# Edge counts by (source block, target) keys in a two-layer graph kernel: pairs of 32-target windows in place of single 64-target windows

## The chip, the cores and the metric

The kernel runs on one core of one Trainium2 chip. The metric is the device time of one execution in microseconds (us). Differences of about 0.2% are what a measurement of this kernel can tell from no change.

## The reference, cut to what matters

There are 1024 nodes with 512 features and 16384 edges `src -> dst`, sorted by `dst`. The targets are drawn as 1024·u², so low numbers of `dst` are the crowded ones; `src` is uniform.

```python
h = relu(layernorm(x))
adj = zeros((N, N)).at[src, dst].set(1)
a = (h @ Wq + bq) @ (h @ Wk + bk).T / sqrt(512)
x = x + softmax(a * adj + (1 - adj) * -1e6) @ (h @ Wv + bv)

h = relu(layernorm(x)) @ W1 + b1
deg = 1 + number of edges per dst;  dinv = deg ** -0.5      # loops included
agg(h)[s] = sum over edges and loops s -> d of dinv[s] * dinv[d] * h[d]
h = relu(batchnorm(agg(h), over nodes)) @ W2 + b2
x = x + agg(h)
```

Both layers need the N x N matrix of edge counts: the first as a mask with sources as rows, the second as the matrix of the aggregations, with targets on the contraction side.

## The kernel before, in words

**Counting.** The edges lie as 128 chunks of 128. The targets are cut into NW = 16 windows of WIN = 64, taken in `ORDER` (14, 15, 0, 1, ... 13). Since edges are sorted, a window needs a run of chunks, whose bounds the program computes into the table `lohi` and reads into a register (`value_load`, L660 on VectorE and L1010 on TensorE). For each chunk VectorE makes two one-hot tiles: `src_oh` (128 edges x 512 columns, L668; a source of 512 and over is told apart by its other tile) and `dst_oh` (L670, three chunks in one instruction: 2 x 64 columns, by half of the sources and target in the window). TensorE multiplies them and adds in PSUM (L1018). A **round** is three chunks (UNROLL) and fills one of 4 ring slots; a window is one lead round of two chunks and then a loop (`Fori`) of rounds whose number is known only from the register. `dst_oh` is compared against `drel`, one table for each window, which GpSimd makes (L355). ScalarE moves a finished window from PSUM to `cnt16` (targets as partitions) in two instructions, which sum the degrees as they go.

With these edges there are 149 chunk visits in 55 rounds: 16 lead rounds and 39 loop rounds. Window i = 2 (targets 0 to 63, "the big window" below) has the lead round and 11 loop rounds; windows i = 3 to 15 have 13 lead and 26 loop rounds.

**Items.** While counting goes on, TensorE also makes "items": h transposed, v, q, and others. The table `ahead` says which items stand before which window. An item is made in a PSUM bank by TensorE, its high part is copied by ScalarE, and VectorE writes the low part (`lo_of`, L651, L647). Matrix products are done as three passes (L948, L949, L950) of high and low parts.

**Attention and W1.** For 8 tiles of 128 sources: scores on TensorE, mask by `copy_predicated` (L768) over `adj`, a DMA transpose of `cnt16` through two rotating buffers, softmax, p split in two halves and transposed by DMA, p times v (`weighted_v`), second layer norm, times W1 (`times_w1`). `dinv` is computed by GpSimd (L314) right after counting.

**Aggregation and W2.** The counts are copied to f32 tiles `cnt` and multiplied with h in agg1 (L1119); batch statistics (L914 to L918), ReLU and the low part of z (L885); z times W2; agg2 (L1196). W2 has a tile of its own, `w2`, loaded by SP (L252) at the beginning of attention and split by ScalarE (L414) and VectorE (L636) near its end.

Each engine's instructions stand in a written order, with semaphores between engines; nothing is reordered by a scheduler.

## Time and profile before

| | before |
|---|---|
| median of 3 runs (lowest, highest) | 311.49 us (311.35, 312.01) |
| profiled execution | 311.82 us |
| its span | 309.8 us |
| mean granted TensorE clock | 0.999 |
| TensorE matmuls busy | 295.1 us (95%) |
| VectorE busy | 210.2 us (68%) |
| ScalarE busy | 143.6 us (46%) |
| GpSimd busy | 55.4 us (18%) |

The profiled execution's time is 2.0 us above its span: what lies before the first and after the last recorded instruction. Times below are us from the start of the span, and a "q" behind an engine's name (DVEq) is its sequencer: it runs the register, branch and table-reading instructions and hands the others on. Such instructions don't count as busy. DVE is VectorE, PE TensorE, ACT ScalarE, POOL GpSimd, SP the engine that issues most DMAs.

### The profile page before, as it was taken

To read this page: it belongs to the slowest core of one execution; us is meant where nothing else is said; L and a number is where in the kernel's file an instruction comes from. 1 tells how busy PE (TensorE), PEld (TensorE's weight loads), DVE (VectorE), ACT (ScalarE), POOL (GpSimd) and SP (SyncE) were. 2 spreads that over 40 slices of the span, in tenths; PEclk is the share of its full clock that TensorE was granted. 3 is DMA by queue.
4 is the path that set the end of the run, shared out by engine and by line. 5 is a ranking of instruction groups with operands and counts; after the bars stand their busy time and mean duration, and the time that the engine had idled before them with its cause. 6 is when DMAs were issued, how large, how long until landed. Compare 5 with 4: busy or idle time off the path is not lost.

```text
span 309.8 us, 4740 instructions
## 1 busy us (share of the span) xinstructions
PE 295.1 (95%) x1319; PEld 227.4 (73%) x1319; DVE 210.2 (68%) x470; ACT 143.6 (46%) x245; POOL 55.4 (18%) x96
## 2 busy tenths in 40 slices
PE   2999969899999999999999999999999999999995
PEld 2977436565666688888888888888788888888884
DVE  3787999999997747667647575757444288376311
ACT  1799944443445626635465445437632035233000
POOL 5234280000000170032121212203010043100000
PEclk9999999999999999999999999999999999999999
DMA  7707040000420127832834636133203000000221
GB/s 268 291 3 204 1 135 0 3 0 0 150 57 3 33 36 107 200 85 53 136 69 102 135 46 124 36 68 59 44 0 70 1 0 2 0 0 2 101 103 68
DMA packets 42310, 21.65 MB, mean 70 GB/s; under 512 B 35760, under 2 KB 36016, under 8 KB 42288
## 3 DMA queue, kind: packets, MB, share of 16 engines
q1 hardware_dynamic: 41744, 20.33, 26.9%
q10 hardware_dynamic: 544, 1.05, 0.9%
q8 instruction: 11, 0.18, 0.2%
q14 instruction: 11, 0.09, 0.1%
HBM read 10.88 MB, written 2.10 MB: 42 GB/s over the span
## 4 chain that ended last, share of the span: by engine, by line
PE 79%; DVE 10%; issue 4%; DVEq 4%; DMA 1%; ACT 1%; SPq 0%; ACTq 0%
PE ps L948 18%; PE ps L950 18%; PE ps L949 18%; PE ps L1196 9%; PE ps L1119 8%; PE ps L1018 5%; DVE src_oh L668 4%; PE ps L986 2%; DVEq L668 2%; DVE dst_oh L670 2%; DMA edge_i<-src_in 1%; DVE hT L651 1%; DVEq L670 1%; DVEq L660 0%; DVEq L674 0%
## 5 line engine op out<-in xcount | busy, mean ns | idle before, releaser
L668 DVE TENSOR_SCALAR src_oh<-iota,ecol 128x512 f16 x149 | 44.2, 346 | 4.0 <-issue 2.9
L1018 PE MATMUL ps<-src_oh,dst_oh 128*128 x149 | 37.9, 382 | 5.4 <-DVE dst_oh L670 4.6
L1018 PEld LDWEIGHTS ps<-src_oh,dst_oh 128*128 x149 | 14.4, 103 | 25.6 <-issue 16.7
L1119 PE MATMUL ps<-cnt,qh 128*128 128x512 f32 x128 | 30.1, 391 | 0.3 <-ACT cnt L541 0.3
L1196 PE MATMUL ps<-qh,cnt 128*128 128x512 f32 x128 | 29.3, 390 | 0.0
L443 ACT ACTIVATE cnt<-ps 64x512 int16<-64x512 f32 x32 | 18.9, 592 | 20.7 <-PE ps L1032 20.3
L1119 PEld LDWEIGHTS ps<-cnt,qh 128*128 128x128 f32 x128 | 23.9, 188 | 5.6 <-DVE qh L827 0.7
L1196 PEld LDWEIGHTS ps<-qh,cnt 128*128 128x128 f32 x128 | 23.9, 188 | 5.2 <-DVE vb L929 0.3
L950 PE MATMUL ps<-v,pT 128*128 128x512 f32 x64 | 25.0, 390 | 0.0
L948 PE MATMUL ps<-v,pT 128*128 128x512 f32 x64 | 24.9, 390 | 0.0
L949 PE MATMUL ps<-v,pT 128*128 128x512 f32 x64 | 24.9, 390 | 0.0
L948 PE MATMUL ps<-hT,qh 128*128 128x512 f32 x64 | 24.9, 389 | 0.0
L949 PE MATMUL ps<-hT,qh 128*128 128x512 f32 x64 | 24.9, 389 | 0.0
L950 PE MATMUL ps<-hT,qh 128*128 128x512 f32 x64 | 24.9, 389 | 0.0
L382 POOL TENSOR_SCALAR lnb<-bnag 128x1 f32<-128x1 f32 x8 | 8.2, 1028 | 82.2 <-DVE bnag L801 82.2
L941 DVE SCALAR_TENSOR_TENSOR xt<-ps,dinv,x 128x512 f32<-128x512 f32 x8 | 5.7, 747 | 17.1 <-PE ps L1196 17.1
L790 DVE TENSOR_SCALAR pT<-p16T 128x1024 fp32r<-128x1024 f16 x8 | 5.5, 693 | 15.9 <-DMA p16T<-p 15.8
L768 DVE COPY_PREDICATED T<-adj,ps 128x1024 f32<-128x1024 int16 x8 | 10.6, 1322 | 7.8 <-PE ps L950 7.8
L525 ACT ACTIVATE hnT<-h16T 128x512 fp32r<-128x512 f16 x8 | 5.1, 632 | 23.2 <-DMA h16T<-h 23.2
L497 ACT ACTIVATE T<-T,smx 128x1024 f32<-128x1024 f32 x8 | 9.2, 1150 | 13.1 <-DVE smx L773 13.1
L466 ACT ACTIVATE T<-zerob,fill 128x1024 f32<-128x1024 bf16 x8 | 9.1, 1147 | 11.9 <-DVE p L780 11.9
L670 DVE TENSOR_TENSOR dst_oh<-iota_w,drel_first 128x384 f16 (+1 forms) x35 | 14.4, 411 | 0.0
(176 smaller groups left out, 658.8 us busy)
## 6 DMA issues: line engine op xcount, KB each, us to landing
xt<-x_in SPq DMA_DIRECT2D x16, 256.0 KB, 3.3
out<-xt SPq DMA_DIRECT2D x8, 256.0 KB, 2.1
qk_raw<-L_gnn_Wk_in ACTq DMA_DIRECT2D x2, 512.0 KB, 4.9
qk_raw<-L_gnn_Wq_in SPq DMA_DIRECT2D x2, 512.0 KB, 6.7
wB_raw<-L_gnn_Wv_in SPq DMA_DIRECT2D x2, 512.0 KB, 8.9
wB_raw<-L_gnn_W_in SPq DMA_DIRECT2D x2, 512.0 KB, 4.3
w_raw<-L_gnn_W_in SPq DMA_DIRECT2D x2, 512.0 KB, 4.8
bias_row<-L_gnn_b_in SPq DMA_DIRECT2D x2, 256.0 KB, 3.7
```

Of the source, the lines that this page charges most:

```text
L443: act.activation(cnt16[rows, a * KC:(a + 1) * KC, w // 2, :], ps[a * WIN:(a + 1) * WIN, i % 2, :].rearrange("p (s n) -> p s n", n=P), ACT. ...
L466: act.activation(T[:, t % 2, :], zerob[:, 0:1].to_broadcast([P, N]), ACT.Identity, bias=fill[:, t:t + 1]).then_inc(S["mask_set"], 1)
L497: act.activation(T[:, t % 2, :], T[:, t % 2, :], ACT.Exp, bias=smx[:, 1, t:t + 1], scale=SCALE, accum_out=smx[:, 2, t:t + 1]).then_inc(S[" ...
L668: dve.tensor_scalar(src_oh[:, bass.ds(slot, 1), j, :].rearrange("p a n -> p (a n)"), iota[:, :], ecol[:, bass.ds(c + j, 1)], None, ALU.is_ ...
L670: dve.tensor_tensor(dst_oh[:, bass.ds(slot, 1), :, 0:count].rearrange("p a n u -> p (a n) u"), iota_w[:, :, 0:count], drel(i)[:, bass.ds(c ...
L768: dve.copy_predicated(T[:, t % 2, :], adj[:, t % ADJ, :], ps[:, 2 * (t % 2):2 * (t % 2) + 2, :].rearrange("p a n -> p (a n)")).then_inc(S[ ...
L948: pe.matmul(out_, stat(1), mov(0), start=first, stop=False)
L949: pe.matmul(out_, stat(0), mov(1), start=False, stop=False)
L950: return pe.matmul(out_, stat(0), mov(0), start=False, stop=last)
L1018: m = pe.matmul(ps[:, i % 2, :], dst_oh[:, bass.ds(slot, 1), :, j].rearrange("p a n -> p (a n)"), src_oh[:, bass.ds(slot, 1), j, :].rearra ...
L1119: m = pe.matmul(bank(g), qh[:, d, a, c * P:(c + 1) * P], cnt[:, d, n * HALF:(n + 1) * HALF], start=(d == 0 and a == 1), stop=last)
L1196: m = pe.matmul(bank(t), cnt[:, d, t * P:(t + 1) * P], qh[:, d, a, :], start=(d == 0 and a == 1), stop=last)
```

## The change

Windows become 32 targets wide, two of them form a pair, and a pair takes the place of a window (NW = 16 pairs, in the same order). The moving tile of a chunk is now `key_oh`, 128 x 256: key = (block of 128 sources) x 32 + target in the window, made with a subtraction and a comparison in one instruction. The stationary tile is `src_oh`, the source's place in its block, 128 columns for each of three chunks. There is no lead round, and no table `drel`; each of a pair's two windows has a loop of its own and bounds of its own. Each pair is moved by one ScalarE instruction of 128 x 512 into `cntT`, with sources as partitions, and the mask reads that directly. For the aggregations eight DMA transposes turn `cntT` into `cntD`. Degrees are summed by eight ScalarE instructions over `cntD` in tiles 1 and 2, and `deg`, the added loops and the flag follow on VectorE in tiles 3 to 5; `dinv` comes on GpSimd ahead of the third `ln2_coef`. W2 shares `wB` with Wv and W1, so it is loaded only when the last product with W1 is done, and is split behind that. The ring has 8 slots.

With the same edges there are now 183 chunk visits in 61 rounds, all of three chunks in loops: 4 in pairs i = 0 and 1, 12 in pair i = 2, and 45 in pairs i = 3 to 15.

```diff
-WIN = 64
-NW = N // WIN
-LEAD = 2
+WIN = 32
+NWIN = N // WIN
+PAIR = 2
+NW = NWIN // PAIR
+BLK = 8
+KEYS = BLK * WIN
 UNROLL = 3
 PAD = 4
-ROUNDS = NW * (2 + NCH // UNROLL)
-RING = 4
+ROUNDS = NWIN * (2 + NCH // UNROLL)
+RING = 8
...
+             [("q", 0, 1)], [("q", 0, 2), ("w", 0, 0)], [("q", 0, 3)], [], []]
...
-                sp.wait_ge(S["c16"], 2 * NW)
-            if t >= ADJ:
-                sp.wait_ge(S["masked"], t - ADJ + 1)
-            sp.dma_start_transpose(adj[:, t % ADJ, :].rearrange("p (b n) -> p b n", b=NT),
-                                   cnt16[:, t, :, :].rearrange("p b n -> p (b n)")).then_inc(
-                S[f"adj_in{t % ADJ}"], 16)
+                sp.wait_ge(S["c16"], NW)
+                sp.wait_ge(S["fill_ready"], 1)
+            sp.dma_start_transpose(cntD[:, :, t, :], cntT[:, t, :]).then_inc(S["turned"], 16)
...
+            if t == 0:
+                for u in range(KC, NT):
+                    turn_counts(u)
...
-            if t == 0:
-                load_w(2)
...
+        sp.wait_ge(S["w1_ps"], NT)
+        load_w(2)
...
+            if t == 2:
+                pool.wait_ge(S["deg_ready"], 1)
+                pw(dinv[:, :], deg[:, :], NT).then_inc(S["dinv_ready"], 1)
...
-            w = ORDER[i]
-            rows = slice(w % 2 * WIN, (w % 2 + 1) * WIN)
+            targets = slice(PAIR * WIN * ORDER[i], PAIR * WIN * (ORDER[i] + 1))
             act.wait_ge(S["c_done"], i + 1)
-            for a in range(2):
-                act.activation(cnt16[rows, a * KC:(a + 1) * KC, w // 2, :],
-                               ps[a * WIN:(a + 1) * WIN, i % 2, :].rearrange("p (s n) -> p s n", n=P), ACT.Copy,
-                               accum_out=degp[rows, a, w // 2:w // 2 + 1]).then_inc(S["c16"], 1)
+            act.activation(cntT[:, :, targets].rearrange("p b (w t) -> p w b t", w=PAIR),
+                           ps[:, i % 2, :].rearrange("p (w b t) -> p w b t", w=PAIR, b=BLK), ACT.Copy).then_inc(S["c16"], 1)
...
+        def degrees(blocks):
+            act.wait_ge(S["turned"], 16 * NT)
+            for b in blocks:
+                act.activation(cntD[:, b, :, :], cntD[:, b, :, :], ACT.Copy,
+                               accum_out=degp[:, b:b + 1]).then_inc(S["deg_sums"], 1)
...
+                degrees(range(KC))
...
+                degrees(range(KC, NT))
...
+        split_w(2)
...
+        step(dve.tensor_scalar(dst_low[:, :], edge_i[:, 0, :], WIN - 1, None, ALU.bitwise_and))
+        step(dve.scalar_tensor_tensor(out=steps[:, 0, :], in0=dst_low[:, :], scalar=1.0 / BLK - 1.0, in1=edge_i[:, 0, :],
+                                      op0=ALU.mult, op1=ALU.add))
...
+        step(dve.tensor_scalar(src_low[:, :], edge_i[:, 1, :], P - 1, None, ALU.bitwise_and))
+        step(dve.scalar_tensor_tensor(out=steps[:, 1, :], in0=src_low[:, :], scalar=-1.0, in1=edge_i[:, 1, :],
+                                      op0=ALU.mult, op1=ALU.add))
+        dve.scalar_tensor_tensor(out=edge_f[:, 0, :], in0=steps[:, 1, :], scalar=float(WIN) / (P * BLK), in1=steps[:, 0, :],
+                                 op0=ALU.mult, op1=ALU.add)
+        dve.tensor_copy(edge_f[:, 1, :], src_low[:, :]).then_inc(S["edge_f_ready"], 1)
...
         def bounds_of(i):
-            return dve.value_load(lohi[0:1, ORDER[i]:ORDER[i] + 1], min_val=256, max_val=257 * NCH)
...
+            return [dve.value_load(lohi[0:1, win:win + 1], min_val=256, max_val=257 * NCH)
+                    for win in (PAIR * ORDER[i], PAIR * ORDER[i] + 1)]
         def onehots(i, bounds):
...
+            for a in range(PAIR):
+                win = PAIR * ORDER[i] + a
+                with dve.Fori(bounds[a] & (NCH - 1), bounds[a] >> 8, UNROLL) as c:
+                    k = dve.snap(made, min_val=0, max_val=ROUNDS)
+                    slot = k & (RING - 1)
+                    dve.wait_ge(S["onehots_used"], k + 1)
+                    for j in range(UNROLL):
+                        dve.tensor_scalar(key_oh[:, bass.ds(slot, 1), j, :].rearrange("p a n -> p (a n)"), iota[:, :],
+                                          kcol[:, bass.ds(c + j, 1)], -float(KEYS * win), ALU.subtract, ALU.is_equal)
+                    dve.tensor_tensor(src_oh[:, bass.ds(slot, 1), :, :].rearrange("p a n u -> p (a n) u"), iota_s[:, :, :],
+                                      scol[:, bass.ds(c, UNROLL)].rearrange("p (o u) -> p o u", o=1).to_broadcast(
+                                          [P, P, UNROLL]), ALU.is_equal).then_inc(S["onehots"], 1)
+                    dve.reg_add(made, made, 1)
...
+        def degrees():
+            dve.wait_ge(S["deg_sums"], NT)
+            dve.tensor_scalar(deg[:, :], degp[:, :], 1.0, None, ALU.add).then_inc(S["deg_ready"], 1)
+            dve.wait_ge(S["deg_ready"], 1)
+            dve.tensor_reduce(degm[:, 0:1], deg[:, :], AX.X, ALU.max).then_inc(S["degm_ready"], 1)
...
-            dve.copy_predicated(T[:, t % 2, :], adj[:, t % ADJ, :],
+            dve.copy_predicated(T[:, t % 2, :], cntT[:, t, :],
...
+            if i == 3:
+                degrees()
+            if i == 4:
+                for b in range(NT):
+                    add_loops(b)
+            if i == 5:
+                large_flag()
...
+            if i == 3:
+                act.wait_ge(S["dinv_ready"], 1)
...
+        split_w(2, 0)
+        split_w(2, 1)
...
-            return pe.value_load(lohi[0:1, ORDER[i]:ORDER[i] + 1], min_val=256, max_val=257 * NCH)
...
+            return [pe.value_load(lohi[0:1, win:win + 1], min_val=256, max_val=257 * NCH)
+                    for win in (PAIR * ORDER[i], PAIR * ORDER[i] + 1)]
         def counts(i, bounds):
             if i >= 2:
-                pe.wait_ge(S["c16"], 2 * (i - 1))
...
+                pe.wait_ge(S["c16"], i - 1)
+            pe.matmul(ps[:, i % 2, 0:32], zerob[:, :], zerob[:, 0:32], start=True, stop=False, skip_group_check=True)
+            for a in range(PAIR):
+                with pe.Fori(bounds[a] & (NCH - 1), bounds[a] >> 8, UNROLL):
+                    k = pe.snap(used, min_val=0, max_val=ROUNDS)
+                    slot = k & (RING - 1)
+                    pe.wait_ge(S["onehots"], k + 1)
+                    for j in range(UNROLL):
+                        m = pe.matmul(ps[:, i % 2, a * KEYS:(a + 1) * KEYS],
+                                      src_oh[:, bass.ds(slot, 1), :, j].rearrange("p a n -> p (a n)"),
+                                      key_oh[:, bass.ds(slot, 1), j, :].rearrange("p a n -> p (a n)"), start=False,
+                                      stop=False, skip_group_check=True)
+                    m.then_inc(S["onehots_used"], 1)
+                    pe.reg_add(used, used, 1)
```

On VectorE, at the head of the first window (before) or pair (after); `lohi` is the table of bounds, ISA and REGISTER_ALU are register instructions, the tiles are the one-hot tiles above. Before:

```order
L660 TENSOR_LOAD lohi
L660 ISA x2
L664 ISA [waits drel_ready]
L668 REGISTER_ALU [waits onehots_used]
L668 ISA
L668 REGISTER_ALU
L668 ISA
L668 TENSOR_SCALAR src_oh<-iota,ecol 128x512
```

After:

```order
L651 TENSOR_LOAD lohi
L651 ISA x2
L651 TENSOR_LOAD lohi
L651 ISA x2
L658 REGISTER_ALU
L658 UNCONDITIONAL_BRANCH
L658 ISA
L663 REGISTER_ALU [waits onehots_used]
L663 ISA
L663 TENSOR_SCALAR key_oh<-iota,kcol 128x256
```

Bounds are read twice in place of once, the wait for `drel` is gone, and the one-hot tiles begin inside a loop. On VectorE, the body of such a loop, one round. Before:

```order
L668 REGISTER_ALU [waits onehots_used]
L668 ISA
L668 TENSOR_SCALAR src_oh<-iota,ecol 128x512
L668 ISA
L668 TENSOR_SCALAR src_oh<-iota,ecol 128x512
L668 ISA
L668 TENSOR_SCALAR src_oh<-iota,ecol 128x512
L670 ISA
L670 TENSOR_TENSOR dst_oh<-iota_w,drel_first 128x384
L674 ISA
L681 COMPARE_AND_BRANCH
```

After:

```order
L663 REGISTER_ALU [waits onehots_used]
L663 ISA
L663 TENSOR_SCALAR key_oh<-iota,kcol 128x256
L663 ISA
L663 TENSOR_SCALAR key_oh<-iota,kcol 128x256
L663 ISA
L663 TENSOR_SCALAR key_oh<-iota,kcol 128x256
L665 ISA
L665 TENSOR_TENSOR src_oh<-iota_s,scol 128x384
L668 ISA
L658 COMPARE_AND_BRANCH
```

The instructions are the same in number and kind, with half the columns in three of them. On VectorE, between the last product with W1 and the first aggregation result (`w` is `w2`, `vb` and `qh` are the parts of h that agg1 reads, `flag` tells of large counts). Before:

```order
L808 TENSOR_SCALAR hnT<-h16T 128x512 [waits w1_ps,h16_lo_in]
L636 TENSOR_TENSOR w<-w_raw,w 128x1024 [waits w_hi] x2
L822 TENSOR_TENSOR vb<-ps,bias_row 128x512 [waits w1_ps]
L827 SCALAR_TENSOR_TENSOR qh<-vb,dinv,qh 128x512 [waits h1_hi]
L889 TENSOR_LOAD flag [waits flag_ready]
```

After:

```order
L792 TENSOR_SCALAR hnT<-h16T 128x512 [waits w1_ps,h16_lo_in]
L806 TENSOR_TENSOR vb<-ps,bias_row 128x512 [waits w1_ps]
L811 SCALAR_TENSOR_TENSOR qh<-vb,dinv,qh 128x512 [waits h1_hi]
L627 TENSOR_TENSOR wB<-wB_raw,wB 128x1024 [waits w_hi] x2
L874 TENSOR_LOAD flag [waits flag_ready]
```

The split of W2 stands behind the last of h and ahead of everything that takes agg1's results.

## Rows read from the trace of the kernel before

**Rows 1.** The profile's page, section 4: the chain that ended last, by engine.

```profile
PE 79%; DVE 10%; issue 4%; DVEq 4%; DMA 1%; ACT 1%; SPq 0%; ACTq 0%
```

**Rows 2.** Stretches of the span: length, busy time (instructions) by engine, TensorE clock, DMA.

```profile
45.00:104.00 59.00, 56.36 (x260) 35.53 (x260) 56.08 (x178) 27.87 (x67) 0.51 (x1) 1.00 0.08 28
104.20:306.50 202.30, 202.01 (x891) 165.65 (x889) 118.49 (x196) 82.71 (x105) 34.79 (x53) 1.00 0.30 63
```

**Rows 3.** Timeline of TensorE at counting's end: start, length, line, out<-in, count [idle].

```profile
103.45 0.82 PE L1018 MATMUL ps<-src_oh,dst_oh 128*128 x3 [0.41 <-DVE dst_oh L670]
...
104.20 0.47 PE L948 MATMUL ps<-hT,M 128*128 128x512 f32 x1
```

**Rows 4.** VectorE's sequencer, all of two lines: ns min/median/max, first and last start.

```profile
L668 DVEq FUSED_REGOPS  x165: 53/93/117, 14.6 to 101.6; - x165
...
L681 DVEq COMPARE_BRANCH  x39: 43/56/75, 16.4 to 102.0; - x39
```

**Rows 5.** Chain of waits inside the big window: start, length, what held the chain.

```profile
29.68 0.31 DVEq L660
...
30.33 0.05 DVEq L664
...
32.66 0.09 DVEq L668
```

**Rows 6.** Timeline of VectorE while counting (columns as in rows 3).

```profile
30.79 0.62 DVE L668 TENSOR_SCALAR src_oh<-iota,ecol 128x512 f16 x2 [0.79 <-issue]
...
31.63 0.88 DVE L668 TENSOR_SCALAR src_oh<-iota,ecol 128x512 f16 x3
...
38.58 0.88 DVE L668 TENSOR_SCALAR src_oh<-iota,ecol 128x512 f16 x3
...
43.58 1.03 DVE L668 TENSOR_SCALAR src_oh<-iota,ecol 128x512 f16 x3
...
45.01 0.65 DVE L668 TENSOR_SCALAR src_oh<-iota,ecol 128x512 f16 x2
...
56.59 0.68 DVE L651 TENSOR_TENSOR v<-ps,v 128x512 fp32r<-128x512 f32 x1
...
58.64 0.86 DVE L668 TENSOR_SCALAR src_oh<-iota,ecol 128x512 f16 x3
...
59.77 0.86 DVE L668 TENSOR_SCALAR src_oh<-iota,ecol 128x512 f16 x3
...
102.77 0.41 DVE L670 TENSOR_TENSOR dst_oh<-iota_w,drel_second 128x384 f16 x1
```

**Rows 7.** Timeline of TensorE inside a window.

```profile
61.23 0.83 PE L1018 MATMUL ps<-src_oh,dst_oh 128*128 x3 [0.30 <-DVE dst_oh L670]
```

**Rows 8.** Timeline of GpSimd beside the big window.

```profile
39.81 5.70 POOL L355 TENSOR_SCALAR drel_second<-dcol 128x132 f16<-128x132 f16 x8
```

**Rows 9.** Timelines in attention: VectorE's low half of p, TensorE's next product.

```profile
162.85 0.69 DVE L790 TENSOR_SCALAR pT<-p16T 128x1024 fp32r<-128x1024 f16 x1 [3.05 <-DMA p16T<-p]
...
164.53 0.39 PE L948 MATMUL ps<-v,pT 128*128 128x512 f32 x1
```

**Rows 10.** Loads and splits of the weights in wB.

```profile
L414 ACT ACTIVATE wB<-wB_raw x4: 1046/1047/1049, 17.2 to 119.4; 128x1024 fp32r<-128x1024 f32 x4
...
DMA to landing us min/median/max: 3.8/6.6/9.2
```

**Rows 11.** VectorE before and in the batch statistics.

```profile
235.26 2.35 DVE L636 TENSOR_TENSOR w<-w_raw,w 128x1024 fp32r<-128x1024 f32 x2
...
246.05 0.69 DVE L914 TENSOR_TENSOR g<-ps,T 128x512 f32<-128x512 f32 x1 [4.57 <-PE ps L1119]
...
258.06 1.23 DVE L885 TENSOR_TENSOR zT<-g,zT 128x1024 fp32r<-128x1024 f32 x1
```

**Rows 12.** TensorE: last aggregation group's start, second quarter of the W2 product.

```profile
239.04 2.21 PE L1119 MATMUL ps<-cnt,qh 128*128 128x512 f32 x9
...
259.45 0.40 PE L948 MATMUL ps<-w,zT 128*128 128x512 f32 x1
```

More of the change, by code:

```diff
@@ L286, in turn_h2 @@
             sp.dma_start_transpose(h16T[:, part, :, :], h16[:, part, :]).then_inc(S[landed], 16)
-        for t in range(ADJ):
+        for t in range(KC):
             turn_counts(t)
@@ L351, in ln1 @@
             pool.tensor_tensor(lnc[:, 3, p], lnc[:, 0, p], lnc[:, 2, p], ALU.mult).then_inc(S["ln_coef"], 2)
-        def targets_of(i):
-            pool.tensor_scalar(drel(i), dcol[:, :], float(-WIN * ORDER[i]), 0.0, ALU.add, ALU.add).then_inc(S["drel_ready"], 1)
-        pool.wait_ge(S["ecol_ready"], 1)
-        pool.wait_ge(S["pad_ready"], 1)
-        for i in range(3):
-            targets_of(i)
-        ln1(0)
-        ln1(2)
-        for i in range(3, 8):
-            targets_of(i)
-        ln1(4)
-        ln1(6)
-        for i in range(8, NW):
-            targets_of(i)
-        pool.wait_ge(S["deg_ready"], 1)
-        pw(dinv[:, :], deg[:, :], NT).then_inc(S["dinv_ready"], 1)
+        for t in range(0, NT, 2):
+            ln1(t)
         def add_bv(t):
@@ L644, in lo_of @@
             if what == "w":
[L645 removed]
+                times_w_row((0, 1)).then_inc(S["item_lo"], 1)
             elif what == "q":
@@ L676, in onehots @@
-        def onehots(i, bounds):
-            first, end = bounds & (NCH - 1), bounds >> 8
-            dve.wait_ge(S["drel_ready"], i + 1)
-            chunks_of(i, first, LEAD)
-            with dve.Fori(first + LEAD, end, UNROLL) as c:
-                chunks_of(i, c, UNROLL)
+            return [dve.value_load(lohi[0:1, win:win + 1], min_val=256, max_val=257 * NCH)
+                    for win in (PAIR * ORDER[i], PAIR * ORDER[i] + 1)]
+        def onehots(i, bounds):
+            for a in range(PAIR):
[11 more added lines that the diff above has]
+                    dve.reg_add(made, made, 1)
@@ L702, in times_w_row, with mask_level @@
             return ins
[L704 to L712 removed]
+        def mask_level():
+            step(dve.tensor_scalar(hw[:, 1, :], hw[:, 0, :], bqbk[:, 0:1], -1.0, ALU.add, ALU.mult))
+            dve.tensor_scalar(fill[:, :], hw[:, 1, :], NEG / SCALE, None, ALU.add).then_inc(S["fill_ready"], 1)
         early = list(start)
@@ L722, in _ @@
         dve.wait_ge(S["lim_ps"], 1)
-        dve.tensor_scalar(lohi[0:1, :], bank(0)[0:1, 0:NW], float(NCH), None, ALU.add).then_inc(S["bounds_ready"], 1)
+        dve.tensor_scalar(lohi[0:1, :], bank(0)[0:1, 0:NWIN], float(NCH), None, ALU.add).then_inc(S["bounds_ready"], 1)
         for item in early[4:6]:
@@ L746, in _ @@
                 columns_of_biases(K if i < 8 else Q, (0, 1) if i % 2 == 0 else (2, 3))
-        for i in range(NW - 2, NW):
-            for item in ahead[i]:
-                lo_of(item)
-        mask_level(slice(0, KC))
-        dve.wait_ge(S["c16"], 2 * NW)
-        step(dve.scalar_tensor_tensor(out=deg[:, :], in0=degp[:, 0, :], scalar=1.0, in1=degp[:, 1, :], op0=ALU.add,
-                                      op1=ALU.add))
-        dve.tensor_reduce(degm[:, 0:1], deg[:, :], AX.X, ALU.max).then_inc(S["degm_ready"], 1)
-        dve.sem_inc(S["deg_ready"], 1)
-        lo_of(("q", 1, 0))
+            if i == NW - 1:
+                times_w_row((2, 3))
+        times_w_row((4, 5))
+        step(times_w_row((6, 7)))
+        mask_level()
+        lo_of(("q", 1, 0))
+        dve.wait_ge(S["c16"], NW)
+        def degrees():
[3 more added lines that the diff above has]
+            dve.tensor_reduce(degm[:, 0:1], deg[:, :], AX.X, ALU.max).then_inc(S["degm_ready"], 1)
         def large_flag():
```

144 lines of the change are left out of this document (40 added, 104 removed).

## The prediction, on record before the changed kernel ran

> **What bounds the kernel now.** I read the chain by engine first: TensorE holds 79% of it, VectorE with its sequencer 14% [rows 1]. The table of stretches says where each counts: from 104.20 to 306.5 TensorE is busy for 202.01 of 202.30 us, at a granted clock of 1.00 (the 2.4 GHz level), so nothing there waits; from 45 to 104 TensorE shows 56.36 and VectorE 56.08 busy of 59.00 [rows 2]. So the time is the end of counting plus a block of gapless matmuls. Counting ends where TensorE's last round, begun at 103.45 after an idle of 0.41 for VectorE's tile, hands over to the q item at 104.20 [rows 3]. What the change does to the time is what it does to 104.20, and any hole that it opens behind it.
>
> Busy shares don't say what paces a counting round; the chain inside the big window does. It runs through VectorE's sequencer, with a register operation ahead of each tile [rows 5]. A loop round has five fused register operations of 93 ns, an ALU operation of 40 and a branch of 56 [rows 4], 0.56 us together, and the rest is handing over. Rounds begin at 31.63 and, six later, at 38.58 [rows 6]: 1.157 apart. Their tiles need less: with queued work behind items, rounds begin at 58.64 and 59.77, 1.13 apart [rows 6], which is execution alone. The two are so close that a busy VectorE looks like the limit and its sequencer hides under it.
>
> **The change, step by step.** All sums are against the profiled execution, 311.82.
>
> *Edge preparation.* Two more small VectorE instructions ahead of the first transposes, some 0.15 each: +0.3 (0 to +0.6).
>
> *A round.* The loop body has the same instructions, only three of them half as wide. If the sequencer paces it, nothing is won: 1.157. If execution did, one wide tile's share is (0.88 − 0.34)/2 = 0.27, its half is 0.13, and a fixed part keeps it above that; with 0.20 a round is 1.13 − 3 × 0.07 = 0.92, and the bounds are 0.72 and 1.13. I take 1.157, because the chain passes the sequencer in every step. It is one of the two things that decide the forecast.
>
> By the perf-mode tier table of the Trainium skill's page "VectorE: DVE Perf Modes", a tensor_scalar on 16-bit SBUF data runs at four elements a cycle, so 256 columns fewer would save about 0.07 us a tile, an estimate; 61 rounds of three would give back 12 us if tiles set the pace. By the section Sequencer Loop of "Advanced Engine Details and Errata" (the Trainium skill) other engine instructions can be read and queued while a control instruction runs, which would favour that too; the chain of [rows 5] shows them in series, and I go by it.
>
> *The big window.* Before it took from 30.79 to 45.01 [rows 6], 14.2 us: a lead round, then eleven, the last ones slower (tiles 1.03 in place of 0.88 a group at 43.58) while GpSimd makes `drel` from 39.81 on [rows 6, 8]. GpSimd's part goes. Now 12 × 1.157 = 13.9 and a second loop entry: −0.2. Ahead of it each pair's bounds are read twice. One reading is what lies from 29.68 to 30.33 [rows 5], 0.65 with nothing beside it. Of four more readings up to there two lie where VectorE waits for weights or x anyway and two do not: +1.3 (0 to 2.6).
>
> *Windows i = 3 to 15.* Before: 45.01 to the last tile at 103.19 [rows 6], 58.2 us for 26 loop and 13 lead rounds, 12 readings and 22 tiles of items of about 0.6 (the row at 56.59 with its successor at 57.19 is one). By the sequencer alone these were about 26 × 1.157 + 13 × 1.0 + 12 × 0.65 = 51, by execution 26 × 1.13 + 13 × 0.86 + 13.4 = 54; the 58.2 is above both, since each took its turn. After: 45 × 1.157 = 52.1, 24 × 0.65 = 15.6, and 1.7 for 26 loop entries and the hand-over of the items: 69.4. Execution would be 45 × 0.92 + 13.4 = 54.8, 14 below, so now the sequencer hides it and I add nothing for turns. +11.2. Bounds: if both still took turns as before, +4 more; if readings hid under items, 7.8 less.
>
> *TensorE behind it.* A round there followed VectorE with an idle of 0.30 at 61.23 [rows 7], so its own sequencer needs at most 1.1; it too reads bounds twice. In windows with item matmuls it falls back by a round, and I let its last round end 2.1 us behind VectorE's last tile in place of 0.9: +1.2 (0 to 2). The longer ring allows that lag and does not shorten it. ScalarE evicts once in place of twice; it is waited for by the pair after next, so that is worth nothing.
>
> Counting ends 0.3 + 1.3 − 0.2 + 11.2 + 1.2 = 13.8 us later, at about 118.
>
> *Attention.* The mask no longer waits for a transposed `adj`; nothing on TensorE waited there [rows 2], so that is worth nothing. Eight transposes stand in SP's queue ahead of and just behind the first of p, ScalarE gets eight degree sums of about 1.15 into its idle time, GpSimd `dinv` one coefficient in front. The tightest place: VectorE's low half of p ends at 163.54 for a product at 164.53 [rows 9], so 1.0 of slack, against 0.75 for `deg` and the wait that ScalarE's h makes for `dinv`. 0 (to +1.5).
>
> *W2.* The load is now issued when the last W1 product ends, 239.04 [rows 12], and everything of it was long hidden before. Landing took between 3.8 and 9.2 in `wB_raw` [rows 10]; the long one shared the DMA engines with x and Wq, and nothing is beside this one, so 4.2: the first half at 243.5. ScalarE 1.05 [rows 10], VectorE 2 × 1.2 [rows 11] in series: 246.9. Queued behind that on VectorE is the first aggregation result, begun at 246.05 before [rows 11]; from there VectorE and ScalarE run at their own pace. The second low part of z ended at 259.29 for TensorE at 259.45 [rows 11, 12], a slack of 0.16. 0.85 late leaves a hole of 0.7 (0 to 2.5; a landing of 9.2 would make it 5.5).
>
> Sum: 311.82 + 13.8 + 0.7 = 326.3. The median of the runs shown is 0.3 below the profiled one: **326.0**.
>
> **Rivals.**
>
> *Tiles pace a round after all.* The place is the loop body: if VectorE's sequencer was only held up by tiles it had queued, halving them frees it. For: rounds behind items already run at 1.13, equal to execution, and in [rows 5] the chain touches tiles as well. Against: 1.157 in the big window, where VectorE was not behind. The price: windows i ≥ 3 at 54.8, −3.4; the big window at 12 × 0.92 + 0.2, −3.0; then +0.3, +1.3, W2's 0.7 and 0.7 of lag: 308. It decides from a round of about 0.98 down; at 1.05 the kernel is already 4 slower. This is the case on the other side: faster, 7 in 100, with up to 311.5 at its edge (same, 3 in 100).
>
> *Readings are hidden.* The second value is read while tiles of the first loops are executed: 14 × 0.65 less on the path, of which I give 6: 320. For: item tiles lie at the same place. Against: 0.65 of chain in [rows 5] for one. 10 in 100.
>
> *TensorE falls to its lower clock.* Its matmuls of 256 columns will be busy for about a third of a round in the big window, where 512 columns filled 0.83 of 1.16. The clock was 1.00 in each stretch [rows 2], so no row here prices the 1.2 GHz level. If the items' matmuls after it ran at the lower level for a few us, they would take twice as long: +1.5 to +4, 330. "TensorE: Matmul & The Clock Gate" of the Trainium skill (section on HAM oscillation) has waits between groups of matmuls lower the clock; by it the sum would be that 330. 10 in 100.
>
> *The subtraction costs VectorE its speed.* `key_oh` needs two operations, and no row shows a two-operation tile of this kind. At one element a cycle in place of the present rate a tile of 256 would take about 0.4 (the 128 x 384 tile of L670 takes 0.41 [rows 6]), a round 3 × 0.4 + 0.33 = 1.53: 57 rounds × 0.37 = +21: 347. 4 in 100.
>
> **How the numbers follow.** My case has 66 in 100, with 322 to 330 as its own range: readings ±2, turns up to +4, W2 from −0.7 to +1.8. The range that should hold 8 in 10 reaches down to partly hidden readings together with a round of 1.10, 316, and up to the clock's case with turns, 333. Faster than before by over 0.2% (about what a measurement of this kernel can tell): 7 in 100; within it: 3; slower: 90.
>
> **What the changed profile would show.** Counting's last matmul near 118; 61 rounds, in the big window 1.15 apart while their tiles are busy for under 0.95 and VectorE shows idle time in front of each round, put down to issue; two table readings of 0.65 in front of each pair. After that the same 202 us of matmuls, with a hole under 1 us at the second quarter of W2's product. VectorE's busy share while counting falls well below 95% although counting takes longer. I am wrong in the first step if rounds stand below 1.0 apart, in the second if TensorE shows no lag from readings, in the third if the clock in the windows is below 0.99, in W2 if the first aggregation result begins later than 248 plus the shift.

## The result, and the profile after

| | before | after |
|---|---|---|
| median (lowest, highest) | 311.42 us (311.3, 312.01) | 333.12 us (332.3, 333.54) |
| ratio, 95% interval | | 1.069 (1.0664 to 1.0715) |
| profiled execution, its span | 311.82, 309.8 us | 332.3, 330.5 us |
| granted TensorE clock | 0.999 | 0.959 |
| last matmul of counting is followed by the q item at | 104.20 us | 122.58 us |
| from there to the end of the span | 205.6 us | 207.9 us |

The kernel is 7% slower. I forecast slower, 326.0; the measured 333.1 is 7 us above that and at the very edge of the range: 0.1 above its upper end of 333, less than the runs of one kernel differ by. Of 20.7 us in the spans, 18.4 come before the q item and 2.3 behind it.

From the page of the profile after: the clock by slices, the chain by engine, and the two costliest groups of counting (busy, mean ns of one | idle before).

```profile
PEclk9999858999997878999999999999999999999999
...
PE 68%; DVE 12%; issue 7%; DVEq 6%; ACT 4%; POOL 1%; DMA 1%; SPq 0%; ACTq 0%; POOLq 0%
...
L663 DVE TENSOR_SCALAR key_oh<-iota,kcol 128x256 f16 x183 | 43.7, 296 | 14.7 <-issue 8.4
L1007 PE MATMUL ps<-key_oh,src_oh 128*128 x183 | 35.4, 309 | 17.4 <-DVE src_oh L665 14.1
```

TensorE holds 68% of the chain where it held 79 [rows 1], "issue" and DVEq 13% where they had 8. The key tiles are shorter than the source tiles were, 296 ns for 346, but 14.7 us of idle stand before them, where there were 4.0. And the clock row has 5, 7 and 8 where each digit was 9.

Stretches of the profile after (columns as in rows 2): counting, one item in it, and the first item behind it.

```profile
45.00:104.00 59.00, 47.32 (x235) 32.44 (x235) 51.73 (x175) 12.37 (x21) 4.99 (x4) 0.93 0.08 28
47.20:52.20 5.00, 5.00 (x14) 3.90 (x13) 4.05 (x16) 0.60 (x1) 0.00 (x0) 0.53 0.00 0
122.58:127.45 4.87, 4.87 (x15) 3.81 (x13) 2.21 (x8) 0.60 (x1) 0.00 (x0) 0.55 0.28 54
```

In 59 us of counting VectorE is busy for 51.7 (56.1 before) and TensorE for 47.3 (56.4) [rows 2]: both idle more, and counting takes longer. That fits a sequencer at its limit; experiments 3 and 4 test it. VectorE's timeline in and behind the big window:

```profile
32.34 0.68 DVE L663 TENSOR_SCALAR key_oh<-iota,kcol 128x256 f16 x3 [1.70 <-issue]
...
39.33 0.68 DVE L663 TENSOR_SCALAR key_oh<-iota,kcol 128x256 f16 x3
...
45.17 0.68 DVE L663 TENSOR_SCALAR key_oh<-iota,kcol 128x256 f16 x3
45.76 0.42 DVE L665 TENSOR_TENSOR src_oh<-iota_s,scol 128x384 f16 x1
47.62 0.68 DVE L663 TENSOR_SCALAR key_oh<-iota,kcol 128x256 f16 x3 [1.43 <-PE ps L1007]
```

The rounds from 32.34 to 39.33 are 1.165 apart, with tiles busy for 0.68 of the 0.88 before [rows 6]. Between 46.18 and 47.62 there are no tiles: the two readings, from 45.9 to 47.1 on the sequencer, stand there. Behind items, rounds are 0.92 apart: this is the execution of one round, as the prediction put it, and the sequencer reaches it only with work queued. The readings themselves, all 32:

```profile
L651 DVEq TENSOR_LOAD <-lohi x32: 297/302/554, 12.4 to 113.3; - x32
```

What I had not seen coming is this stretch of VectorE's timeline, and GpSimd's beside it:

```profile
95.48 0.67 DVE L663 TENSOR_SCALAR key_oh<-iota,kcol 128x256 f16 x3
...
98.00 3.07 DVE L663 TENSOR_SCALAR key_oh<-iota,kcol 128x256 f16 x3 [0.92 <-PE ps L1007]
101.00 1.50 DVE L665 TENSOR_TENSOR src_oh<-iota_s,scol 128x384 f16 x1
102.41 0.67 DVE L663 TENSOR_SCALAR key_oh<-iota,kcol 128x256 f16 x3
...
103.33 0.67 DVE L663 TENSOR_SCALAR key_oh<-iota,kcol 128x256 f16 x3
...
112.22 0.75 DVE L638 SCALAR_TENSOR_TENSOR qh<-ps,uw,qh 128x512 fp32r<-128x512 f32 x1 [1.84 <-ACT qh L433]
...
120.29 0.43 DVE L665 TENSOR_TENSOR src_oh<-iota_s,scol 128x384 f16 x1
```

```profile
97.23 4.99 POOL L355 TENSOR_TENSOR xt<-xt,bias_row 128x512 f32<-128x512 f32 x4 [59.15 <-DMA bias_row<-L_gnn_bv_in]
```

Three key tiles take 3.07 us in place of 0.68, and the next tile 1.50 in place of 0.42: the round from 98.00 to 102.41 takes 4.41. They run beside GpSimd's four additions of bv, the bias of Wv, to x (L355). In the kernel before, GpSimd waited for the degrees ahead of them, and they ran from 108.82 on, behind counting; with `dinv` moved back, nothing holds them until bv has landed.

TensorE's timeline at a few places:

```profile
37.13 0.60 PE L1007 MATMUL ps<-key_oh,src_oh 128*128 x3 [0.51 <-DVE src_oh L665]
...
38.29 0.82 PE L1007 MATMUL ps<-key_oh,src_oh 128*128 x3 [0.56 <-DVE src_oh L665]
...
46.45 0.82 PE L1007 MATMUL ps<-key_oh,src_oh 128*128 x3 [0.30 <-DVE src_oh L665]
...
48.22 0.63 PE L935 MATMUL ps<-wB,hT 128*128 128x512 f32 x1
...
66.22 0.60 PE L1007 MATMUL ps<-key_oh,src_oh 128*128 x3 [0.55 <-DVE src_oh L665]
...
102.76 0.86 PE L1007 MATMUL ps<-key_oh,src_oh 128*128 x3 [2.02 <-DVE src_oh L665]
...
121.84 0.82 PE L1007 MATMUL ps<-key_oh,src_oh 128*128 x3 [0.28 <-issue]
...
122.58 0.77 PE L933 MATMUL ps<-hT,M 128*128 128x512 f32 x1
```

A round of three 256-column matmuls takes 0.60 at the clock's upper level and 0.82 at its lower one, 1.2 GHz; a matmul of an item 0.39 or 0.63. In the big window TensorE is idle for 0.5 to 0.6 ahead of the rounds at 35.97, 37.13 and 38.29, and the last of these is the first at the lower level. The round at 102.76, after 2.02 of idle beside the stretched round, is at the lower level too. The four rounds around 66.22, which stand between items, have as much idle ahead of them and stay at the upper level. The granted clock is 0.53 and 0.55 over the two stretches of items above. The q item at 122.58 then takes 4.87 us where it took 2.80 (104.20 to 107.00 before).

W2, VectorE's and TensorE's timelines:

```profile
264.21 2.58 DVE L627 TENSOR_TENSOR wB<-wB_raw,wB 128x1024 fp32r<-128x1024 f32 x2 [2.09 <-ACT wB L394]
266.70 0.68 DVE L899 TENSOR_TENSOR g<-ps,T 128x512 f32<-128x512 f32 x1
```

```profile
259.69 2.66 PE L1100 MATMUL ps<-cnt,qh 128*128 128x512 f32 x11
```

The split of W2 ends with the start of the first aggregation result at 266.70, 7.01 us behind 259.69. Before it was 246.05 behind 239.04 [rows 11, 12], also 7.01. The late load costs nothing here, and nothing is to spare: the aggregation result begins as the split ends.

### The profile page after: what moved, and what is told of

Read it like the earlier page. It is cut to its first block, busy times and chain, and to the rows that moved or that the text cites. A ratio compares the mean times of both kernels' runs of the same rounds, so it can differ in the third digit from the quotient of the medians.

```text
span 330.5 us, 5138 instructions
## 1 busy us (share of the span) xinstructions
PE 301.3 (91%) x1369; PEld 235.3 (71%) x1369; DVE 216.2 (65%) x511; ACT 138.2 (42%) x213; POOL 46.9 (14%) x80
## 4 chain that ended last, share of the span: by engine, by line
PE 68%; DVE 12%; issue 7%; DVEq 6%; ACT 4%; POOL 1%; DMA 1%; SPq 0%; ACTq 0%; POOLq 0%
PE ps L933 16%; PE ps L934 15%; PE ps L935 15%; PE ps L1177 9%; PE ps L1100 8%; DVE key_oh L663 5%; PE ps L1007 3%; DVEq L663 3%; DVE src_oh L665 2%; DVEq L651 2%; PE ps L971 2%; DMA edge_i<-src_in 1%; ACT T L408 1%; DVEq L658 1%; POOL lnc L343 1%
## 5 line engine op out<-in xcount | busy, mean ns | idle before, releaser
L663 DVE TENSOR_SCALAR key_oh<-iota,kcol 128x256 f16 x183 | 43.7, 296 | 14.7 <-issue 8.4
L1007 PE MATMUL ps<-key_oh,src_oh 128*128 x183 | 35.4, 309 | 17.4 <-DVE src_oh L665 14.1
L1007 PEld LDWEIGHTS ps<-key_oh,src_oh 128*128 x183 | 18.1, 104 | 31.5 <-issue 26.9
L665 DVE TENSOR_TENSOR src_oh<-iota_s,scol 128x384 f16 x61 | 26.8, 439 | 0.0
L421 ACT ACTIVATE cntT<-ps 128x512 int16<-128x512 f32 x16 | 9.5, 602 | 39.2 <-PE ps L1013 39.2
L355 POOL TENSOR_TENSOR xt<-xt,bias_row 128x512 f32<-128x512 f32 x8 | 10.2, 1297 | 68.8 <-DMA bias_row<-L_gnn_bv_in 59.1
L933 PE MATMUL ps<-wB,hT 128*128 128x512 f32 x32 | 14.1, 441 | 1.3 <-DVE hT L642 1.3
L752 DVE COPY_PREDICATED T<-cntT,ps 128x1024 f32<-128x1024 int16 x8 | 10.5, 1316 | 6.3 <-PE ps L935 6.3
```

The costliest lines, as they stand in the source:

```text
L355: pool.tensor_tensor(xt[:, n % XT, :], xt[:, n % XT, :], bias_row[:, 0, :], ALU.add).then_inc(S["xb_ready"], 1)
L421: act.activation(cntT[:, :, targets].rearrange("p b (w t) -> p w b t", w=PAIR), ps[:, i % 2, :].rearrange("p (w b t) -> p w b t", w=PAIR, ...
L663: dve.tensor_scalar(key_oh[:, bass.ds(slot, 1), j, :].rearrange("p a n -> p (a n)"), iota[:, :], kcol[:, bass.ds(c + j, 1)], -float(KEYS * ...
L665: dve.tensor_tensor(src_oh[:, bass.ds(slot, 1), :, :].rearrange("p a n u -> p (a n) u"), iota_s[:, :, :], scol[:, bass.ds(c, UNROLL)].rear ...
L752: dve.copy_predicated(T[:, t % 2, :], cntT[:, t, :], ps[:, 2 * (t % 2):2 * (t % 2) + 2, :].rearrange("p a n -> p (a n)")).then_inc(S["mask ...
L933: pe.matmul(out_, stat(1), mov(0), start=first, stop=False)
```

## The experiments

Ten kernels, in three sets on one chip each; beside each set ran the kernel before (311.67, 311.62 and 311.49 us). "End of counting" is the start of the q item behind it, and "tail" what lies from there to the end of the span. The timelines are of one profiled execution of each kernel.

**1. Additions held back** (`a_hold`), the changed kernel with

```diff
+        pool.wait_ge(S["c16"], NW)
         for t in range(XT):
             add_bv(t)
```

> The changed kernel, with GpSimd's first four additions of bv held until the last pair is counted. My theory: in the changed kernel these additions (97.2 to 102.2 us) run beside VectorE's one-hot tiles and stretch one round from about 1 to 4.4 us; held back, that round takes 1.0 to 1.2 and the time falls by 3 to 4.5 us, from 333.1 to 329 to 330. Rival: the round is stretched by the load of W1 or bv that lands near there, or by TensorE; then it stays stretched and the time stays at 333.

Measured: 328.25 us (327.84 to 329.17), 4.9 less and 0.75 below what I expected; end of counting 119.13, 3.45 earlier. Of the two profiled executions, one is the shortest of the changed kernel's and the other the longest of this one's, so their spans differ by 3.2 only. VectorE's and GpSimd's timelines:

```profile
98.16 0.68 DVE L664 TENSOR_SCALAR key_oh<-iota,kcol 128x256 f16 x3 [0.90 <-PE ps L1008]
...
99.34 0.68 DVE L664 TENSOR_SCALAR key_oh<-iota,kcol 128x256 f16 x3 [0.17 <-issue]
...
117.55 0.41 DVE L666 TENSOR_TENSOR src_oh<-iota_s,scol 128x384 f16 x1
...
119.72 0.68 DVE L687 SCALAR_TENSOR_TENSOR hrow<-hrow,w_row 128x512 f32<-128x512 f32 x1
...
120.33 1.75 DVE L687 SCALAR_TENSOR_TENSOR hrow<-hrow,w_row 128x512 f32<-128x512 f32 x1
```

```profile
119.96 6.21 POOL L355 TENSOR_TENSOR xt<-xt,bias_row 128x512 f32<-128x512 f32 x4 [81.70 <-ACT cntT L422]
```

The rounds at 98.16 and 99.34 are ordinary, so the rival, a load that lands near there, is out: only the additions were moved. The item behind them no longer runs at the lower clock, and VectorE's wait of 1.84 for it is gone. VectorE's last tile ends at 117.96 for 120.72. At 120.33, where the additions now run, a product of a row of h with `w_row` (from these products the level of the mask is made) takes 1.75 us in place of 0.68, and the four additions take 6.21 in place of 4.99: the two engines hold each other up there too.

**2. TensorE kept busy** (`a_fill`), the changed kernel with, behind each round's matmuls,

```diff
+                    for j in range(2):
+                        pe.matmul(ps[:, i % 2, :], zerob[:, :], zerob[:, 0:1].to_broadcast([P, HALF]), start=False,
+                                  stop=False, skip_group_check=True)
```

> The changed kernel, with two more matmuls of 512 columns of zeros behind each counting round on TensorE (they add zero to the counts). My theory: the granted clock of 0.96 comes from rounds in which TensorE is busy for 0.6 of 1.16 us; filled, the clock is 0.99 or above in every stretch, the items behind a window run at 0.23 a matmul throughout, and the time falls by 3 to 4 us, to 329 to 330. Rival: the clock costs nothing, since VectorE's sequencer sets the end of counting anyway: then only the first q item behind the counting is shorter, 2 us, to 331. Second rival: the added matmuls make TensorE the slower one, and the time rises.

Measured: 331.04 us (330.28 to 331.72), 2.1 less, with a clock of 1.00. A stretch of counting, VectorE's last tile, and the q item:

```profile
45.00:61.00 16.00, 15.67 (x90) 10.55 (x90) 12.45 (x48) 3.37 (x6) 0.00 (x0) 1.00 0.01 2
```

```profile
118.97 0.41 DVE L665 TENSOR_TENSOR src_oh<-iota_s,scol 128x384 f16 x1
```

```profile
122.26 0.48 PE L933 MATMUL ps<-hT,M 128*128 128x512 f32 x1
```

The stretch had a clock of 0.79 in the changed kernel. Yet counting ends only 0.3 us earlier, and the time is that of the first rival. It hides two things, though. VectorE's last tile ends 1.3 earlier (119.38 for 120.72), since its wait behind the item after the stretched round is 0.42 in place of 1.84; and the added matmuls keep TensorE busy behind that tile, so that the q item follows 2.88 us after it in place of 1.86. So the lower clock costs where something waits for TensorE's own work, at that one item and in the q item; in the rounds themselves no cost of it shows.

**3. Key tiles 512 wide** (`a_wide`), the changed kernel with

```diff
-RING = 8
+RING = 4
-("key_oh", [P, RING, UNROLL, KEYS], BF16)
+("key_oh", [P, RING, UNROLL, HALF], BF16)
-("iota", [P, KEYS], F16)
+("iota", [P, HALF], F16)
...
-key_oh[:, bass.ds(slot, 1), j, :]            # TensorE's operand
+key_oh[:, bass.ds(slot, 1), j, 0:KEYS]
```

> The changed kernel, with key tiles written 512 columns wide (only 256 are read) and 4 ring slots in place of 8. My theory: a round is paced by VectorE's register operations, so most of the 61 rounds stay at 1.16 us and only the ten or so that run behind items, 0.92 apart now, go to 1.13: +1 to +3 us, 334 to 336. Rival: the tiles' execution paces the rounds; then 0.07 us for each of 183 tiles comes on top, +12 us, 345.

Measured: 332.96 us (332.23 to 333.06): 0.2 less, below what I expected. VectorE's timeline, in the big window and behind items:

```profile
32.65 0.88 DVE L663 TENSOR_SCALAR key_oh<-iota,kcol 128x512 f16 x3
...
33.82 0.88 DVE L663 TENSOR_SCALAR key_oh<-iota,kcol 128x512 f16 x3
...
103.19 0.86 DVE L663 TENSOR_SCALAR key_oh<-iota,kcol 128x512 f16 x3
...
104.32 0.86 DVE L663 TENSOR_SCALAR key_oh<-iota,kcol 128x512 f16 x3
```

Twice the columns, and a round in the big window is 1.17 as ever; behind items it is 1.13 in place of 0.92. (The ring of 4 goes with the wide tiles, for room.) From the first tile of the big window, here at 31.46 for 32.34, to the end of counting, 123.85, it is 92.4 us for 90.2: +2.2, as the theory had it. That the time did not rise is chance: the first tile came 0.9 earlier, and the tail was 1.4 shorter, 206.6, since the q item ran less at the low clock. This is the plainest evidence of all: 183 tiles of double width cost counting 2.2 us, where tiles that pace the rounds would cost 12.

**4. The columns alone, in the kernel before** (`b_narrow`)

```diff
-dve.tensor_scalar(src_oh[:, bass.ds(slot, 1), j, :] ..., iota[:, :],
+dve.tensor_scalar(src_oh[:, bass.ds(slot, 1), j, 0:HALF // 2] ..., iota[:, 0:HALF // 2],
...
-src_oh[:, bass.ds(slot, 1), j, :] ...           # TensorE's operand
+src_oh[:, bass.ds(slot, 1), j, 0:HALF // 2].to_broadcast([P, 2, HALF // 2])
```

> The kernel before with source tiles 256 columns wide; TensorE reads each twice, side by side, so its matmuls stay 512 columns (the counts of half the sources are left out and the others stand in their place). It is the halving of columns alone. My theory: rounds inside a window stay at 1.16, since the sequencer paces them already; only where VectorE runs behind items are 0.2 us a round won, and the turns that both took: 3 to 5 us less, 307 to 309. Rival: the tiles' execution paces the kernel before: 149 tiles by 0.07 or more, 10 us or more less, 301 or below.

Measured: 308.22 us (307.9 to 308.58), 3.4 less than before, ratio 0.990 (0.988 to 0.992), as expected. VectorE's timeline:

```profile
32.30 0.68 DVE L668 TENSOR_SCALAR src_oh<-iota,ecol 128x256 f16 x3 [0.17 <-issue]
...
33.46 0.68 DVE L668 TENSOR_SCALAR src_oh<-iota,ecol 128x256 f16 x3
```

Rounds in the big window are 1.16 apart, as with 512 columns. So this is what narrow tiles are worth in this kernel: 1.1%, and none of it is won in the big window, which takes 14.22 us with either width. Of the 3.9 by which counting ends earlier (100.32), 3.4 are won behind the big window, where VectorE runs behind items.

**5. Each reading twice** (`a_reads2`), on VectorE and on TensorE

```diff
-                    for win in (PAIR * ORDER[i], PAIR * ORDER[i] + 1)]
+                    for win in (PAIR * ORDER[i], PAIR * ORDER[i] + 1) for twice in range(2)][::2]
```

> The changed kernel with each reading of bounds done twice on VectorE and TensorE (64 readings in place of 32). My theory: a reading is 0.65 us on VectorE's sequencer and is hidden only where VectorE has tiles queued; of the 32 added ones the 24 ahead of windows i = 3 and later count nearly in full and 2 to 4 of the earlier ones: +15 to +19 us, 348 to 352. Rival: readings lie beside item tiles and TensorE's matmuls: +0 to +6, below 340.

Measured: 351.19 us (350.37 to 351.81), 18.1 more, as expected. End of counting, TensorE's timeline:

```profile
140.98 0.82 PE L1007 MATMUL ps<-key_oh,src_oh 128*128 x3 [0.28 <-issue]
...
141.73 0.77 PE L933 MATMUL ps<-hT,M 128*128 128x512 f32 x1
```

19.15 later for 32 readings: 0.60 each, nearly the 0.65 of one alone. The first tile of the big window comes at 38.55, 6.2 later for the 8 readings ahead of it; the 24 behind cost 12.9, 0.54 each. Readings are hardly hidden.

**6. Additions held and TensorE kept busy** (`a_hold_fill`), the edits of 1 and 2.

> The changed kernel with both edits at once: GpSimd's additions of bv held until counting is done, and two matmuls of zeros behind each round. My theory: these are the two costs that the prediction's sum lacked, so what is left is that sum: 326 to 327, with a clock of 1.00 and counting's end near 118. Rival: they overlap (the stretched round is what lowers the clock), and nothing is won over holding alone: 328.

Measured: 327.87 us (327.13 to 328.2), clock 1.00, end of counting about 119.8. As the rival says: over holding alone nothing is gained that can be told apart. The fill gives 1.6 back in the tail (206.6 for 208.2). Counting ends 0.7 later, of which 0.4 lie ahead of the big window (its first tile is at 32.96 for 32.52) and 0.2 behind VectorE's last tile; between these two tiles both kernels take 85.44 us, so with the additions held the clock costs VectorE nothing. The two edits together are worth 5.3, less than the 4.9 and 2.1 that they are worth alone: a part of what the stretched round costs is paid through the clock. What stays above the forecast here is 1.9, and nearly all of it is in counting, which ends at 119.8 for the 118 of the forecast.

**7. One window of 64 with 512 keys** (`w64`), the changed kernel with

```diff
-WIN = 32
-PAIR = 2
-RING = 8
+WIN = 64
+PAIR = 1
+RING = 4
...
-                    for win in (PAIR * ORDER[i], PAIR * ORDER[i] + 1)]
+                    for win in range(PAIR * ORDER[i], PAIR * ORDER[i] + PAIR)]
```

> The changed kernel with WIN = 64 and PAIR = 1 (keys of 512, one loop and one reading of bounds for a window, 53 rounds of three, 4 ring slots); mask, transposes, degrees and W2 stay as in the changed kernel. My theory: the loss is in the counting (8 rounds and 16 readings more); here counting ends near 104 to 108 as in the kernel before, TensorE's clock stays at 1.00, and the time is 312 to 316, with GpSimd's additions still stretching a round. Rival: the loss is in what follows counting (transposes in SP's queue, degrees, W2 loaded late): then the time stays above 325.

Measured: 317.32 us (316.6 to 317.86). End of counting 108.46, tail 206.3. 15.8 of the 21.7 us lost come back by this alone, although mask, transposes, degrees and W2 are as in the changed kernel; so most of the loss is in counting. The tail is still 0.7 longer than before. 1.3 above my range's end: here too a round is stretched, from 91.68 to 96.31, beside the additions.

**8. The same, additions held, products moved** (`w64_best`), the kernel of 7 with

```diff
+        pool.wait_ge(S["c16"], NW)              # ahead of add_bv(0)
...
-            if i == NW - 1:
-                times_w_row((2, 3))
-        times_w_row((4, 5))
+        lo_of(("w", 0, 0))                      # in `ahead` the w item stands before the last window again
+        times_w_row((2, 3, 4, 5))
```

> WIN = 64 and PAIR = 1 with GpSimd's additions held and all products of h with the w row behind the last window. My theory: from 317.3 the stretched round gives back 3.3 us and the two products inside counting 2.4: 311 to 313, equal to the kernel before within 0.5%, since it has 53 rounds in place of 55 but ten chunks more. Rival: what followed counting costs something after all (eight transposes, degrees in the tiles, W2 loaded late): then it stays at 314 or above.

Measured: 315.36 us (315.26 to 315.44): 2.0 less than 7, and above what I expected, where the rival had it, but mostly not for the rival's reason (9). Counting ends at 105.37, 3.1 earlier, but the tail is 208.2. VectorE's timeline, and a row of TensorE's waits (us, times, longest):

```profile
105.72 0.69 DVE L687 SCALAR_TENSOR_TENSOR T<-T,w_row 128x512 f32<-128x512 f32 x1
...
106.33 1.78 DVE L687 SCALAR_TENSOR_TENSOR T<-T,w_row 128x512 f32<-128x512 f32 x1
...
108.04 1.77 DVE L687 SCALAR_TENSOR_TENSOR hrow<-hrow,w_row 128x512 f32<-128x512 f32 x1
```

```profile
PE ps L933 <- ACT pT L491: 1.5, 1, 1.5
```

Held until counting is done, the additions (106.21 to 112.67) meet the products with the w row, and four of them take 1.7 us in place of 0.6, from one start to the next. The stall had moved, not gone.

**9. Held until the mask's level is done** (`w64_late`), the kernel of 8 with

```diff
-        pool.wait_ge(S["c16"], NW)
+        pool.wait_ge(S["fill_ready"], 1)
```

> The kernel of w64_best, with GpSimd's additions of bv held until VectorE's products with the w row and the level of the mask are done, in place of until counting is done. In w64_best four of these products take 1.7 us in place of 0.6 beside the additions, and TensorE waits 1.5 us for p later. My theory: the two engines hold each other up whenever they run such instructions side by side; moved behind them, the products take 0.6 us each, TensorE's wait goes, and the time falls by 2 to 3 us to 312.5 to 313.5. Rival: the wait for p comes from the eight transposes ahead of p's in SP's queue; then products shorten and the time stays at 315.

Measured: 313.31 us (313.18 to 314.07), ratio to before 1.0065 (1.0048 to 1.0081), as expected. VectorE's timeline, then GpSimd's from 109.59:

```profile
106.51 0.68 DVE L687 SCALAR_TENSOR_TENSOR hrow<-hrow,w_row 128x512 f32<-128x512 f32 x1
...
107.12 0.68 DVE L687 SCALAR_TENSOR_TENSOR hrow<-hrow,w_row 128x512 f32<-128x512 f32 x1
...
109.34 0.17 DVE L694 TENSOR_SCALAR fill<-hw 128x8 f32<-128x8 f32 x1
...
109.59 5.04 POOL L355 TENSOR_TENSOR xt<-xt,bias_row 128x512 f32<-128x512 f32 x4 [71.73 <-DVE fill L694]
```

Products take 0.61 each, and TensorE's wait for p is gone. The rival, transposes ahead of p's, is out. The best kernel with counts by key is still 1.8 us slower than the one before. Counting ends 0.8 later (104.97), for which its ten chunks more, 159 for 149, are a likely reason; the other 1.0 is in the tail (206.6 for 205.6), where TensorE waits once, 0.17 us, for the low part of z, and the rest wasn't taken apart. So what follows counting does cost something, as the rival of 8 had it: 1.0.

**10. The first loop round written out** (`b_lead`), the kernel before with

```diff
             chunks_of(i, first, LEAD)
-            with dve.Fori(first + LEAD, end, UNROLL) as c:
+            chunks_of(i, first + LEAD, UNROLL)
+            with dve.Fori(first + LEAD + UNROLL, end, UNROLL) as c:
```

and likewise on TensorE.

> The kernel before, with the first loop round of every window taken out of the loop and written behind the lead round (same chunks, same tiles; the 16 first rounds need no branch and no loop register). My theory: with the sequencer near the limit in the kernel before too, 0.1 to 0.2 us less of register work in 16 windows is worth 0 to 2 us, of which most is seen where VectorE is not behind: 310 to 311.5. Rival: a second copy of the body lengthens the program, and loading it costs as much or more: 311.6 or above.

Measured: 316.56 us (316.38 to 316.68), 5.1 more: the theory was wrong, and the rival, whose range holds it, had another reason. From the page:

```profile
L668 DVE TENSOR_SCALAR src_oh<-iota,ecol 128x512 f16 x167 | 49.7, 350 | 4.0 <-issue 2.3
```

There are 167 tiles where there were 149 and 61 rounds for 55: this loop runs once even where its bounds leave nothing, and six windows have only one loop round, which is the one now written out. As an attempt at fewer register operations it says nothing; as a price it does: six more rounds ended counting 4.9 us later (109.10), 0.8 each, in the kernel before.

No version that computes the reference beat the kernel before.

## Why the prediction was right, and where it was short

Numbers in brackets are those of the experiments.

*What bounds the kernel.* Right: the time is the end of counting plus a gapless block, 205.6 before and 205.8 after when the q item's 2.1 at the low clock is taken off.

*A round costs 1.157 whatever its columns.* Right, the step on which the forecast rested. 1.165 in the changed kernel, 1.17 with tiles twice as wide (3), 1.16 with tiles half as wide in the kernel before (4). A tile itself became 0.07 us shorter: from a group of three and a single tile, (0.68 − 0.28)/2 = 0.20 in place of (0.88 − 0.34)/2 = 0.27. By the perf-mode tier table of the Trainium skill's "VectorE: DVE Perf Modes" 256 columns fewer are worth 0.07 us, an estimate; the trace agrees with the page on the tile. It also shows that the tile was not what counted. By the section Sequencer Loop of "Advanced Engine Details and Errata" (the Trainium skill) instructions can be queued while control instructions run. The rounds behind items, 0.92 apart, agree with that; in the big window, where VectorE has no work queued, the register operations still set 1.165.

*Edge preparation and readings ahead of the big window*, +1.6: the first tile came at 32.34 for 30.79, +1.55. So close a match is partly luck: in (1), whose edit does not touch this stage, it came at 32.52, and in the others of this kind between 31.46 (3) and 32.96 (6). *The big window*, −0.2: 13.99 for 14.22, from its first tile to a round behind its last.

*Windows i ≥ 3*, +11.2: mis-sized. From there to the last tile's end it was 46.33 to 120.72, 74.4 for 58.2: +16.2. The 5 that are missing fall into three parts:

- 3.0 hang on GpSimd's additions (1): with them held the term is 117.96 − 46.51 = 71.4. They are the round that is stretched and, behind it, VectorE's wait of 1.84 for ScalarE's q at 110.38, behind an item at the low clock. I had followed `dinv` to its new place on GpSimd and asked who waits for it, but not what it had been holding back: four additions of which I knew the duration, the row they had run in, and that bv lands while counting goes on. The Trainium skill has the rule that would have led there: "SBUF — State Buffer", Who interferes with whom, says that VectorE in its two-port modes and GpSimd share a pair of SBUF ports, which whoever issues first holds for its whole instruction, and that a VectorE instruction with two SBUF inputs contends with a GpSimd one that reads SBUF. The traces agree: a group of key tiles at 3.07 and products of two SBUF inputs at 1.75 beside the additions, and both back to normal when these are moved (1, 9).
- About 1.2 are the first two products with `w_row`, which the change puts ahead of the last pair (from 112.89 to 114.1 on VectorE); I had counted them nowhere. This is read from the timeline; no run moves them alone.
- The remaining 0.8 no run separates. The readings are not it: by (5) a further one costs 0.54 here, less than the 0.65 of the sum; if that holds for each of the 24, what no run separates is larger by 2.6.

*TensorE behind it*, +1.2: from the last tile's end to the q item 1.86 for 1.02, +0.84, within the range given.

*Attention*, 0: right; TensorE shows no wait there. *W2*, +0.7: 0. The landing of the first half took 3.2 where I had taken 4.2, and the 7.01 are unchanged.

*Rivals.* The clock, at 10 in 100, came true on top of the main case, at 1.5 to 4 us as written, 2.1 by (2). I had priced it as a case of its own, while it follows from the same rounds that I took for my main case; the trace has TensorE busy for 0.60 of 1.165 there, about half and not the third that I wrote. It belonged in the sum. The Trainium skill's "TensorE: Matmul & The Clock Gate" (HAM oscillation) describes a clock that falls in waits between groups of matmuls; its waits are for DMAs and longer than the 0.5 us of idle here. What shows the cause in this case is (2), where nothing but the filling changed and the clock was 1.00. Tiles that pace a round (3, 4), hidden readings (0.60 each by (5)) and the slow two-operation tile (0.28 us, where the plain one of twice the width took 0.34) did not happen.

So the mechanism was right and 326 was 7 us short: 5.3 are the additions and the clock together (6), 4.9 the additions alone (1) and 2.1 the clock alone (2), which overlap, and 1.9 is left. That 333.1 still falls at the edge of the range is in part luck: the range's top was reached by turns and the clock's case, neither of which is the additions.

What stays open: the 1.9 by which (6) is above the forecast, of which about 1.2 may be the two products. That execution does not pace a round is shown by widths that change nothing; that it is the sequencer follows from that and from the chain of waits, while no run took register operations away, and which of them matter most wasn't tried.

## What to carry to other kernels

Where an engine looks 95% busy, look at what its sequencer does between the tiles before paying anything for smaller tiles: register operations and branches are paid per round, readings of loop bounds per window, and finer windows add to both (here 61 rounds for 55 and 32 readings for 16). When a wait is moved on one engine, ask what it was holding back, and what that will now run beside. A change that leaves TensorE idle in each round can lower its clock for what comes next, so price that together with the idle time.

## What the runs showed of the hardware that I had not expected

- VectorE and GpSimd hold each other up: three 128x256 tensor_scalar at 3.07 us in place of 0.68, a 128x512 product of two SBUF inputs at 1.75 in place of 0.68, beside additions of 128x512 on GpSimd. GpSimd's four additions took 5.04 us with nothing beside them (9), 4.99 in the changed kernel and 6.21 in (1).
- A tensor_scalar of 256 or 512 f16 columns costs the same in a register-controlled loop of three where VectorE has no work queued: 1.16 to 1.17 us a round. With work queued it is 0.92 for 1.13.
- A dynamic loop whose start is at or past its end still ran once: 61 rounds for the 55 that its bounds ask for.
- TensorE's clock fell to its lower level in the big window, at 38.29, where TensorE had stood idle for 0.5 to 0.6 us ahead of each round. It stayed up in the kernel before, and with zeros added behind each round (2).
